# Cross-attention on one core: two of three value visits of a stage put side by side, and the work behind a visit reordered

## The chip, the core and the metric

The kernel runs on one core of a Trainium2 chip. The metric is device time in microseconds (us), from one launch to its end, as the median of several runs. On the core, TensorE (PE in the profile, its weight loads PEld) multiplies; VectorE (DVE), ScalarE (ACT) and GpSimd (POOL) work beside it; SyncE's queue (SPq) starts the DMAs. Each engine takes its instructions strictly in the order written, and they hold each other back by semaphores alone.

## The reference

A transformer block for 8 batch elements of 224 tokens of width 512, with 16 heads of 32: layer norms, masked self-attention, cross-attention over 750 context tokens, and a feed-forward net, all added to the input. What the change touches is the cross-attention:

```python
xs = _layernorm(src, ln2_g, ln2_b)
kv = xs @ ed_wkv
k2, v2 = (_heads(t) for t in jnp.split(kv, 2, axis=-1))
q2 = _heads(xq @ ed_wq)
wei2 = jnp.einsum('bhtd,bhjd->bhtj', q2, k2) * scale
wei2 = jax.nn.softmax(wei2, axis=-1)
ed_out = _merge(jnp.einsum('bhtj,bhjd->bhtd', wei2, v2)) @ ed_wproj + ed_bproj
result = result + ed_out
```

## The kernel before

Feed-forward and self-attention take about the first 750 us. Behind them comes the cross-attention, written as a plan: a list of named items, made by `plan_cross_attention`. Every engine walks the same list and issues its own part of each item, so the list is the order on all engines at once.

The work is cut into 32 groups of four heads (8 batch elements, 4 groups each). The 750 keys are six tiles of 125, taken as three pairs. The plan runs in stages. Stage s computes the keys of group s (items K), the score products of group s-1 (16 items "score", 112 queries by 376 keys, of which VectorE only takes the maxima, L1664), turns the maxima of group s-2 (M), computes the probabilities of group s-3 (12 items "prob": a head and a pair of key tiles each, two matmuls at L1744, which ScalarE exponentiates at L1607), and finishes group s-4. A stage has 12 slots. Slot i holds prob i, then a score product, then the fill of the slot (half of a K or of a value projection V, three to six matmuls at L1727; a part of an output projection E, three matmuls at L1832 for each; or T, three transposes of the next context, L1819), then further score products. I call a stage by s mod 4. Types 0 to 3 differ in their fill: type 0 has V, K and, from the third batch element on, E in slots 6, 7, 9 and 10, and none in 8 and 11; types 1 and 2 have none in slots 6 and 7 (type 1) or 7 (type 2) and none in 10 and 11; type 3 has a T in each slot from 4 to 11.

A "value visit" (item "value", L1773) multiplies one pair of key tiles with the values: eight matmuls whose results are 32 columns wide, one for each head and tile, four of them side by side in the array (the records show 16, two for each). Everything else in the loop uses 98 to 128 rows and up to 128 columns, M's two transposes apart. The visits of group s-3 stand at the end of slots 7 and 10 and, for the third pair, in slot 3 of the next stage, where the softmax denominators follow (item D, L1791, of the same shape). GpSimd adds up the probabilities for D (L1582, L1586), two additions behind slot 7 and two behind slot 11 of each stage; it also computes the low half of each T (L1473).

Three waits matter. A score product needs the third last user of its three banks to be read (L1757, L1758); a prob needs the exponential before the last (two banks, L1740, L1741); a visit needs its four exponentials (L1764). An E's last part is followed by an addition of the residual on VectorE (L1721), which stands before the maxima of the slot's last score products.

Of the kernel before, what the change touches and what calls it, by code (L numbers as in the profile page):

```python
# [636 lines left out]
def plan_attention(B):  # L637

    other = plan_cross_attention(B)
    start = other.index(FIRST_IN_TURN)  # L640
    early = [item for slot in EARLY.values() for item in slot]
    assert set(early) >= set(other[:start])
    items = []
    for item in plan_self_attention(B):
        if item[0] == "other_stage":
            items += [("ca",) + o for o in EARLY.get(item[1:], ())]
        else:
            items.append(("sa",) + item)
    behind = items.index(("sa", "T_split", 0, 1)) + 1
    items[behind:behind] = [("ff", "last")]  # L650
    return items + [("ca",) + o for o in other[start:] if o not in early]
# [623 lines left out]
VECTOR_SUMS = {3: (2,), 2: (1, 2), 1: (1,)}  # L1275
STATISTICS = ((1, 8), (1, 9), (1, 10), (1, 11), (2, 0), (2, 1))
OFFSET = (2, 3)


def plan_cross_attention(B):  # L1280

    NG = 4 * B
    items, late = [], []
    for s in range(-1, NG + 4):
        g, b = s % 4, s // 4
        fill = {i: [] for i in range(SLOTS)}  # L1290

        def put(slots, item, there):
            for part, i in enumerate(slots):
                if there:
                    fill[i].append(item + (part,))

        keys, now = 0 <= s < NG, 0 <= b < B
        if g == 0:
            put((0, 1), ("V", b, 0), now and b > 0)
            put((2, 3), ("K", s, 0), keys)  # L1300
            put((4, 5), ("K", s, 1), keys)
            put((7, 9), ("V", b, 0), now and b == 0)
            put((6, 6, 7, 7) if keys else (0, 0, 1, 1), ("E", b - 2, 0), 0 <= b - 2 < B - 1)
            put((9, 9, 10, 10), ("E", b - 2, 1), 0 <= b - 2 < B - 2)
        elif g == 1:
            put((0, 1), ("K", s, 0), keys)
            put((2, 3), ("K", s, 1), keys)
            put((4, 5), ("V", b, 1), now and b > 0)
            put((8, 9), ("V", b, 2), now)
        elif g == 2:  # L1310
            put((0, 1), ("K", s, 0), keys)
            put((2, 3), ("K", s, 1), keys)
            put((5, 6), ("V", b, 3), now)
            put((8, 9), ("V", b, 4), now)
        else:
            put((0, 1), ("K", s, 0), keys)
            put((2, 3), ("K", s, 1), keys)
            put((4, 5), ("V", b, 5), now)
            for n in range(8):
                if b + 1 < B:  # L1320
                    fill[4 + n].append(("T", b + 1, n % 4, n // 4))
        for i, c, m, part in LAST_E.get(s - NG, ()):
            fill[i].append(("E", B - c, m, part))
        for i in range(SLOTS):
            scores = []
            if 0 <= s - 1 < NG:
                scores = [("score", s - 1, u) for u in range(SCORED[g][i], SCORED[g][i + 1])]
            if 0 <= s - 3 < NG:
                items.append(("prob", s - 3, i))
            if i == 2 and 0 <= s - 2 < NG:  # L1330
                items.append(("M", s - 2))
            items += scores[:1]
            items += fill[i]
            items += late
            late = [("T_rest",) + item[1:4] for item in fill[i] if item[0] == "T"]
            items += [(item[0] + "_rest",) + item[1:3] for item in fill[i] if item[0] + str(item[3]) in ("K1", "E3")]
            if i == 3 and 0 <= s - 4 < NG:
                items.append(("value", s - 4, 2))
            divided = 3 if s <= NG else LAST_D
            for j, name in enumerate(("D", "", "D_high", "D_low") if s <= NG else ("D", "D_high", "D_low")):  # L1340
                if name and i == divided + j and 0 <= s - 4 < NG:
                    items.append((name, s - 4))
            items += scores[1:]
            if i == SLOTS - 1 and 0 <= s - 1 < NG:
                items.append(("negate", s - 1))
            if i % 4 == 3 and 0 <= s - 3 < NG and (s - 3, i) != (NG - 1, SLOTS - 1):
                items.append(("sum", s - 3, i))
            if i == 3 and keys:
                items.append(("queries", s))
            if i in (7, 10) and 0 <= s - 3 < NG:  # L1350
                items.append(("value", s - 3, (i - 7) // 3))
            if now and b + 1 < B:
                if b > 0 and (g, i) in STATISTICS:
                    items.append(("statistics", b + 1, STATISTICS.index((g, i))))
                if (g, i) == OFFSET:
                    items.append(("offset", b + 1))
                if g == 2:
                    items += [("normalise", b + 1, t) for t in range(CTX_TILES) if NORMALISE[t] == i]
                if (g, i) == (0, 11) and b > 0:
                    items += [("context", b + 1, a) for a in range(2)]  # L1360
        if g == 3 and 1 <= b < B - 1:
            items.append(("weights_low", b + 1))
        if g == 1 and 0 <= b - 2 < B - 1:
            items.append(("store", b - 2))
        if g == 2 and 0 <= b - 1 < B:
            items.append(("result", b - 1))
    return items
# [495 lines left out]
```

## Time and profile before

| | us |
|---|---|
| median of 3 runs | 1369.85 |
| lowest and highest run | 1369.48, 1372.99 |
| the profiled execution, span | 1372.2 |
| TensorE busy in it | 1310.9 |
| VectorE, GpSimd, ScalarE busy in it | 794.4, 701.5, 662.1 |

The rows further down come from the one profiled execution. In a timeline row the columns are: start, time from the start of the first to the end of the last of the instructions merged in it, engine, line, operation, result <- operands, shapes, count, and in brackets the idle time before it with what ended it. A matmul's record begins when it is issued and ends when its result is written, so records of matmuls overlap; two of them are compared here by their ends.

### The profile page before, as it was taken

To read this page: it belongs to the slowest core of one execution; us is meant where nothing else is said; L and a number is where in the kernel's file an instruction comes from. 1 tells how busy PE (TensorE), PEld (TensorE's weight loads), DVE (VectorE), ACT (ScalarE), POOL (GpSimd) and SP (SyncE) were. 2 spreads that over 40 slices of the span, in tenths; PEclk is the share of its full clock that TensorE was granted. 3 is DMA by queue.
4 is the path that set the end of the run, shared out by engine and by line. 5 is a ranking of instruction groups with operands and counts; after the bars stand their busy time and mean duration, and the time that the engine had idled before them with its cause. 6 is when DMAs were issued, how large, how long until landed. Compare 5 with 4: busy or idle time off the path is not lost.

```text
span 1372.2 us, 24578 instructions
## 1 busy us (share of the span) xinstructions
PE 1310.9 (96%) x9193; PEld 1082.5 (79%) x9193; DVE 794.4 (58%) x2007; ACT 662.1 (48%) x1609; POOL 701.5 (51%) x577
## 2 busy tenths in 40 slices
PE   7999999999899999998788999999999999999997
PEld 6888888888788888887677787878877787887874
DVE  6613223232777777776655575756757566575565
ACT  5311111232666665666433656474665647456444
POOL 3232221322444555556733767666676766667661
PEclk9999999999999999999599999999999999999999
DMA  7400102114647776547267685777677587766641
GB/s 237 145 18 16 62 31 77 46 60 117 139 86 178 166 186 148 122 123 185 63 142 119 100 128 98 132 123 125 101 127 120 101 137 104 142 101 112 90 71 41
DMA packets 100400, 151.67 MB, mean 111 GB/s; under 512 B 10197, under 2 KB 63229, under 8 KB 99514
## 3 DMA queue, kind: packets, MB, share of 16 engines
q1 hardware_dynamic: 100282, 150.11, 53.8%
q8 instruction: 73, 1.20, 0.4%
q14 instruction: 45, 0.37, 0.1%
HBM read 66.74 MB, written 24.12 MB: 66 GB/s over the span
## 4 chain that ended last, share of the span: by engine, by line
PE 76%; POOL 8%; issue 5%; DVE 5%; DMA 3%; ACT 2%; SPq 1%; POOLq 0%; ACTq 0%; DVEq 0%
PE ps L1727 18%; PE ps L453 11%; PE ps L164 10%; PE ps L423 10%; PE ps_pair L1744 6%; PE ps L1759 5%; PE ps L1773 5%; PE ps L1832 3%; POOL ca_partial L1586 2%; DMA ca_k_stack<-ca_keys 2%; POOL ca_xT L1473 1%; DMA sa_K_stack<-sa_rows 1%; PE ps L1207 1%; PE ps L1791 1%; PE ps L1227 1%
## 5 line engine op out<-in xcount | busy, mean ns | idle before, releaser
L1664 DVE TENSOR_REDUCE ca_maxes<-ps 112x1 f32<-112x375 f32 x512 | 256.5, 541 | 106.0 <-PE ps L1759 103.9
L1607 ACT ACTIVATE ca_probT<-ps_pair 125x448 f32<-125x448 f32 x384 | 210.3, 554 | 181.5 <-PE ps_pair L1744 179.6
L1586 POOL TENSOR_TENSOR ca_partial<-ca_partial,ca_probT 125x896 f32<-125x896 f32 x118 | 249.2, 2112 | 93.6 <-ACT ca_probT L1607 89.0
L312 POOL TENSOR_TENSOR ff_hT<-ff_hrelu,ff_hT 128x512 fp32r<-128x512 f32 (+1 forms) x64 | 77.9, 1218 | 203.2 <-DVE ff_hT L394 203.2
L1759 PE MATMUL ps<-ca_k_stack,ca_q_stack 96*112 96x376 f32 x512 | 168.7, 352 | 6.9 <-issue 3.6
L1744 PEld LDWEIGHTS ps_pair<-ca_q_stack,ca_k_stack 98*125 98x125 f32 x768 | 130.2, 186 | 44.0 <-issue 31.9
L1744 PE MATMUL ps_pair<-ca_q_stack,ca_k_stack 98*125 98x224 f32 x768 | 156.2, 285 | 1.3 <-ACT ca_probT L1607 1.2
L423 PE MATMUL ps<-ff_w,ff_hT 128*128 128x512 f32 x672 | 155.5, 390 | 0.0
L1727 PE MATMUL ps<-w_b,ca_xT 128*125 128x512 f32 x576 | 151.2, 398 | 3.1 <-POOL ca_xT L1473 2.5
L1727 PE MATMUL ps<-ca_xT,w_a 128*128 128x376 f32 x768 | 153.1, 335 | 0.0
L423 PEld LDWEIGHTS ps<-ff_w,ff_hT 128*128 128x128 f32 x672 | 125.6, 188 | 25.8
L1038 ACT ACTIVATE sa_prob<-sa_prob,sa_maxes 112x112 f32<-112x112 f32 (+1 forms) x256 | 109.2, 428 | 67.0 <-DVE sa_maxes L1112 66.9
L341 ACT ACTIVATE ff_hrelu<-ps,columns 128x512 f32<-128x512 f32 (+1 forms) x64 | 40.7, 636 | 200.9 <-PE ps L453 194.5
L1727 PEld LDWEIGHTS ps<-ca_xT,w_a 128*128 128x128 f32 x768 | 130.3, 189 | 0.6
L1112 DVE CUSTOM_DVE_ANT_0 sa_prob<-ps_pair,sa_masks 112x112 f32<-112x112 f32 (+1 forms) x256 | 74.5, 328 | 87.7 <-PE ps_pair L1197 86.2
L1727 PEld LDWEIGHTS ps<-w_b,ca_xT 128*125 128x125 f32 x576 | 105.7, 188 | 23.3 <-ACT ca_xT_f L1651 3.5
L394 DVE CAST ff_hT<-ff_hrelu 128x512 fp32r<-128x512 f32 (+1 forms) x64 | 27.8, 437 | 147.0 <-ACT ff_hrelu L341 146.8
L1582 POOL TENSOR_TENSOR ca_partial<-ca_probT 125x896 f32<-125x896 f32 x32 | 67.8, 2117 | 71.6 <-PE ps L1791 39.5
L1759 PEld LDWEIGHTS ps<-ca_k_stack,ca_q_stack 96*112 96x112 f32 x512 | 86.3, 177 | 20.0 <-DVE ca_maxes L1664 10.9
L1773 PE MATMUL ps<-ca_probT,ca_v 125*32 125x224 f32 x1536 | 92.6, 359 | 0.6 <-ACT ca_probT L1607 0.6
L1713 DVE TENSOR_TENSOR ca_keys<-ps,ca_keys 128x376 fp32r<-128x376 f32 x64 | 35.2, 550 | 77.5 <-ACT ca_keys L1640 77.5
L155 POOL TENSOR_TENSOR sa_rows<-sa_f,one 128x224 fp32r<-128x224 f32 x64 | 40.3, 629 | 76.0 <-ACT sa_f L1093 61.5
(145 smaller groups left out, 2433.0 us busy)
## 6 DMA issues: line engine op xcount, KB each, us to landing
ca_k_stack<-ca_keys SPq DMA_DIRECT2D x96, 376.0 KB, 8.0
sa_Q_stack<-sa_rows SPq DMA_DIRECT2D x96, 112.0 KB, 3.5
sa_K_stack<-sa_rows SPq DMA_DIRECT2D x96, 112.0 KB, 3.7
ca_q_stack<-q_out SPq DMA_DIRECT2D x96, 112.0 KB, 9.5
ctx_tokens<-in_ctx_dram SPq DMA_DIRECT2D x14, 672.0 KB
ctx_tokens<-in_L_xattn_ff_w_dram SPq DMA_DIRECT2D x16, 512.0 KB, 4.4
q_out<-sa_yT SPq DMA_DIRECT2D x16, 448.0 KB, 3.7
wp_lo<-wp_out SPq DMA_DIRECT2D x6, 1024.0 KB, 4.8
```

The costliest lines, as they stand in the source:

```text
L164: mm = pe.matmul(acc, lhs(a, k), rhs(b, k), start=n == 0, stop=n == len(steps) - 1)
L312: pool.tensor_tensor(hT[:, LO, m % RING, 0:width(g)], hrelu[i % 2][:, 0:width(g)], hT[:, HI, m % RING, 0:width(g)].bitcast(F32), ALU.subtr ...
L423: mm = pe.matmul(ps_y[t], hT[:, a, (KT * c + k) % RING, P * t:P * (t + 1)], w2[c][:, b, k, :], start=(c, k, a, b) == (0, 0) + PASSES[0], s ...
L453: mm = pe.matmul(ps_h[i % 2][:, 0:width(g)], w1[c][:, a, k, P * (m % KT):P * (m % KT + 1)], xT[:, b, k, tokens(g)], start=(k, n) == (0, 0) ...
L1038: ins = act.activation(prob[:, n % 4, TQ * q:TQ + T * q], prob[:, n % 4, TQ * q:TQ + T * q], ACT.Exp, bias=maxes[:, n % 4, q:q + 1], scale ...
L1586: pool.tensor_tensor(total, total, half(a), ALU.add).then_inc(partial_done, 1)
L1607: act.activation(probT[u // GH][0:JT, u % GH].rearrange("p a t -> p (a t)"), ps_p[u % 2][0:JT, 0:2 * T], ACT.Exp).then_inc(exp_done, 1)
L1664: dve.tensor_reduce(maxes[:, q, j, a:a + 1], ps_s[n % 3][0:TQ, 0:JH], AX_X, ALU.max).then_inc(s_read, 1)
L1727: mm = pe.matmul(acc, lhs(a, k), rhs(b, k), start=(k, i) == (0, 0), stop=(k, i) == (3, 2))
L1744: mm = pe.matmul(ps_p[n % 2][0:JT, T * i:T * (i + 1)], k_stack[:, h, t // 3, JT * (t % 3):JT * (t % 3 + 1)], q_stack[:, h, :], start=True, ...
L1759: pe.matmul(ps_s[n % 3][0:TQ, 0:JP], q_stack[0:KS, h, TQ * q:TQ * (q + 1)], k_stack[0:KS, h, a, :], start=True, stop=True).then_inc(s_psum, 1)
L1773: mm = pe.matmul(ps_o[HD * j:HD * (j + 1), 0:T], v[b % 2][:, t, HD * h:HD * (h + 1)], probT[pair][0:JT, j, i], start=t == 0, stop=t == NT - 1)
```

## The change

The first two pairs of key tiles meet the values in one place, at the end of slot 9, one visit directly behind the other. In slots 4 and 10, the slots that now follow visits, the slot's first score product stands ahead of the prob; where a stage has no score products left, the fill would stand there.

```diff
+VALUES_AT = 9
+BEHIND_VALUES = (4, VALUES_AT + 1)
...
-            if 0 <= s - 3 < NG:
-                items.append(("prob", s - 3, i))
-            if i == 2 and 0 <= s - 2 < NG:
-                items.append(("M", s - 2))
-            items += scores[:1]
-            items += fill[i]
+            prob = [("prob", s - 3, i)] if 0 <= s - 3 < NG else []
+            if i in BEHIND_VALUES:
+                items += (scores[:1] or fill[i]) + prob + (fill[i] if scores else [])
+            else:
+                items += prob
+                if i == 2 and 0 <= s - 2 < NG:
+                    items.append(("M", s - 2))
+                items += scores[:1] + fill[i]
...
-            if i in (7, 10) and 0 <= s - 3 < NG:
-                items.append(("value", s - 3, (i - 7) // 3))
+            if i == VALUES_AT and 0 <= s - 3 < NG:
+                items += [("value", s - 3, pair) for pair in range(2)]
```

The order moves on TensorE alone; on the other engines and on SyncE's queue the same instructions stand in the same order. TensorE, a type 0 stage, from the end of slot 7 to slot 11 (L1759 is a score product, L1744 a prob, L1832 a part of E, L1773 a value visit), before:

```order
1295 L1759 MATMUL ps<-ca_k_stack,ca_q_stack 112x376
1296 L1773 MATMUL ps<-ca_probT_112,ca_v_111 32x224 x8
1297 L1744 MATMUL ps_pair<-ca_q_stack,ca_k_stack 125x224 x2
1298 L1759 MATMUL ps<-ca_k_stack,ca_q_stack 112x376 x2
1299 L1744 MATMUL ps_pair<-ca_q_stack,ca_k_stack 125x224 x2
1300 L1759 MATMUL ps<-ca_k_stack,ca_q_stack 112x376
1301 L1832 MATMUL ps<-ca_wp_103,ca_oT_123 112x512
1302 L1832 MATMUL ps<-wp_lo,ca_oT_123 112x512
```

The same place now (all lines of this part of the file are 4 higher: L1763, L1748, L1836 and L1777):

```order
1299 L1763 MATMUL ps<-ca_k_stack,ca_q_stack 112x376
1300 L1748 MATMUL ps_pair<-ca_q_stack,ca_k_stack 125x224 x2
1301 L1763 MATMUL ps<-ca_k_stack,ca_q_stack 112x376 x2
1302 L1748 MATMUL ps_pair<-ca_q_stack,ca_k_stack 125x224 x2
1303 L1763 MATMUL ps<-ca_k_stack,ca_q_stack 112x376
1304 L1836 MATMUL ps<-ca_wp_103,ca_oT_123 112x512
1305 L1836 MATMUL ps<-wp_lo,ca_oT_123 112x512
```

The visit between the last score product of slot 7 and the prob of slot 8 is gone, and four score products follow with two probs between them and no other work.

TensorE, the end of slot 9 and slot 10 of a type 3 stage (L1819 is a T), before:

```order
1249 L1744 MATMUL ps_pair<-ca_q_stack,ca_k_stack 125x224 x2
1250 L1759 MATMUL ps<-ca_k_stack,ca_q_stack 112x376
1251 L1819 MATMUL ps<-ident,ctx_tokens 128x125 x3
1252 L1759 MATMUL ps<-ca_k_stack,ca_q_stack 112x376
1253 L1744 MATMUL ps_pair<-ca_q_stack,ca_k_stack 125x224 x2
1254 L1759 MATMUL ps<-ca_k_stack,ca_q_stack 112x376
1255 L1819 MATMUL ps<-ident,ctx_tokens 128x125 x3
1256 L1759 MATMUL ps<-ca_k_stack,ca_q_stack 112x376
```

The same place now:

```order
1250 L1763 MATMUL ps<-ca_k_stack,ca_q_stack 112x376
1251 L1823 MATMUL ps<-ident,ctx_tokens 128x125 x3
1252 L1763 MATMUL ps<-ca_k_stack,ca_q_stack 112x376
1253 L1777 MATMUL ps<-ca_probT_112,ca_v_111 32x224 x8
1254 L1777 MATMUL ps<-ca_probT_113,ca_v_111 32x224 x8
1255 L1763 MATMUL ps<-ca_k_stack,ca_q_stack 112x376
1256 L1748 MATMUL ps_pair<-ca_q_stack,ca_k_stack 125x224 x2
1257 L1823 MATMUL ps<-ident,ctx_tokens 128x125 x3
```

Both visits now stand between slots 9 and 10, and the score product of slot 10 comes before its prob.

## Rows read from the trace of the kernel before

**Rows 1.** The page: the chain that ended last, share of the span by engine

```profile
PE 76%; POOL 8%; issue 5%; DVE 5%; DMA 3%; ACT 2%; SPq 1%; POOLq 0%; ACTq 0%; DVEq 0%
```

**Rows 2.** Stages of type 3, 0, 1, 2: us, busy by engine, granted clock, DMA share, GB/s

```profile
983.15:1003.41 20.26, 19.50 (x159) 15.55 (x158) 12.09 (x24) 15.20 (x31) 14.70 (x10) 1.00 0.66 96
1003.41:1025.83 22.42, 22.07 (x161) 17.50 (x160) 12.35 (x24) 9.91 (x21) 15.26 (x11) 1.00 0.63 119
1025.83:1045.18 19.35, 19.33 (x149) 15.58 (x148) 12.52 (x25) 8.73 (x19) 11.23 (x6) 1.00 0.94 172
1045.18:1064.05 18.87, 18.87 (x149) 15.42 (x148) 14.42 (x36) 12.29 (x25) 12.57 (x7) 1.00 0.65 91
```

**Rows 3.** Timeline, type 0, TensorE: score then prob; the same around a visit

```profile
1021.78 0.34 PE L1759 MATMUL ps<-ca_k_stack,ca_q_stack 96*112 96x376 f32 x1
1021.96 0.38 PE L1744 MATMUL ps_pair<-ca_q_stack,ca_k_stack 98*125 98x224 f32 x2
...
1023.74 0.33 PE L1759 MATMUL ps<-ca_k_stack,ca_q_stack 96*112 96x376 f32 x1
...
1024.90 0.48 PE L1744 MATMUL ps_pair<-ca_q_stack,ca_k_stack 98*125 98x224 f32 x2
```

**Rows 4.** Timeline, type 1, TensorE: third visit (slot 3) with D behind it

```profile
1030.87 0.96 PE L1773 MATMUL ps<-ca_probT,ca_v 125*32 125x224 f32 x16
...
1031.65 0.56 PE L1791 MATMUL ps<-ca_partial,ca_ones 125*32 125x224 f32 x8
```

**Rows 5.** Timeline, type 0, slots 7 to 9: TensorE and VectorE

```profile
1018.17 0.33 PE L1759 MATMUL ps<-ca_k_stack,ca_q_stack 96*112 96x376 f32 x1
1018.37 0.69 DVE L1721 TENSOR_TENSOR ca_res<-ps,ca_res 112x512 f32<-112x512 f32 x1 [0.79 <-PE ps L1832]
...
1018.98 0.54 DVE L1664 TENSOR_REDUCE ca_maxes<-ps 112x1 f32<-112x375 f32 x1
```

**Rows 6.** Timeline, type 1, slots 6 and 7: VectorE's maxima, slot 7's two score products

```profile
1036.37 2.37 DVE L1664 TENSOR_REDUCE ca_maxes<-ps 112x1 f32<-112x375 f32 x5 [0.75 <-PE ps L1759]
...
1036.97 0.88 PE L1759 MATMUL ps<-ca_k_stack,ca_q_stack 96*112 96x376 f32 x2
```

**Rows 7.** Timeline, type 2, slots 6 and 7: the same

```profile
1056.25 1.46 DVE L1664 TENSOR_REDUCE ca_maxes<-ps 112x1 f32<-112x375 f32 x3 [0.69 <-PE ps L1759]
1056.27 0.50 PE L1759 MATMUL ps<-ca_k_stack,ca_q_stack 96*112 96x376 f32 x2
```

**Rows 8.** Timeline, type 3 and start of type 0: ScalarE, GpSimd, and TensorE behind them

```profile
997.57 0.98 POOL L1473 TENSOR_TENSOR ca_xT<-ca_xT_f,ca_xT 128x375 fp32r<-128x375 f32 x1 [0.22 <-ACT ca_xT_f L1651]
...
998.51 4.28 POOL L1586 TENSOR_TENSOR ca_partial<-ca_partial,ca_probT 125x896 f32<-125x896 f32 x2
...
999.38 0.41 PE L1759 MATMUL ps<-ca_k_stack,ca_q_stack 96*112 96x376 f32 x1
...
1001.91 0.64 ACT L1607 ACTIVATE ca_probT<-ps_pair 125x448 f32<-125x448 f32 x1
...
1003.87 1.63 PE L1727 MATMUL ps<-w_b,ca_xT 128*125 128x512 f32 x6 [0.35 <-POOL ca_xT L1473]
...
1006.53 4.30 POOL L1586 TENSOR_TENSOR ca_partial<-ca_partial,ca_probT 125x896 f32<-125x896 f32 x2
...
1010.89 0.58 PE L1791 MATMUL ps<-ca_partial,ca_ones 125*32 125x224 f32 x8
```

**Rows 9.** Timeline, the last two groups: exponentials on ScalarE, probs and last visit

```profile
1345.13 0.97 ACT L1607 ACTIVATE ca_probT<-ps_pair 125x448 f32<-125x448 f32 x2
...
1348.76 2.77 ACT L1607 ACTIVATE ca_probT<-ps_pair 125x448 f32<-125x448 f32 x5 [0.76 <-PE ps_pair L1744]
...
1355.82 0.48 PE L1744 MATMUL ps_pair<-ca_q_stack,ca_k_stack 98*125 98x224 f32 x2
...
1359.46 0.54 ACT L1607 ACTIVATE ca_probT<-ps_pair 125x448 f32<-125x448 f32 x1 [0.76 <-PE ps_pair L1744]
1360.06 0.96 PE L1773 MATMUL ps<-ca_probT,ca_v 125*32 125x224 f32 x16 [0.63 <-ACT ca_probT L1607]
```

## The prediction

> **What bounds the kernel now.** I read the chain of work that ended last first: three quarters of the span are TensorE's own work [rows 1]. Then busy time by stretch, over one period of the cross-attention, four stages, which repeats itself to some hundredths of a us from the second batch element to the seventh: stages of type 1 and 2 have TensorE busy for all but 0.02 us, type 0 for all but 0.35, type 3 for all but 0.76, with the clock granted in full, its level of 2.4 GHz [rows 2]. So a us taken off TensorE in types 1 and 2 is a us off the time, unless TensorE then waits for somebody. The next view is therefore the timeline around each place where a visit stood: who is late there if the visit is not.
>
> **What a visit costs.** Ends of records are compared. From the end of a score product to the end of the two matmuls of the next prob it takes 0.22 us without a visit (1022.12 to 1022.34) and 1.31 us with one (1024.07 to 1025.38) [rows 3]: a visit costs 1.09. Of this its own streaming is less. D, eight records in two sets of four, ends 0.38 behind the visit ahead of it (1031.83 to 1032.21) [rows 4]: 0.19 a set, and no loss between the two. A visit is four sets, 0.76. So 0.33 are lost around each visit, and a visit that directly follows another costs 0.76. The change takes one such loss from each of the 32 groups: 32 x 0.33 = 10.6 us of TensorE's time. The nearest row to the new edge, visit to visit, is the edge visit to D, same shape [rows 4], and I take it as it is.
>
> The Trainium skill, page "TensorEngine Tiling (Array Packing)", section "Key Properties", says that a change of the tiling mode drains TensorE while a change of tile does not; the trace agrees, with 0.33 lost around a visit and none between visit and D. By that rule alone the change would give all of the 10.6 us, about 1359.3; I weigh it as a rival.
>
> **The two reordered slots.** In slots 4 and 10 the score product goes first. Every matmul's own step depends on itself (score 0.17, a prob 0.22 for its two), and the loss at the end of a visit now falls on another instruction. I find no row with a score product behind a visit; bounds are that all or none of the exit's part of 0.33 goes, at most 0.33 either way for each. I take 0: the prob and what stands behind it end when they did. The prob reaches ScalarE 0.17 later and the score reaches VectorE 0.2 earlier.
>
> **Where the saving is taken back.** A score product waits for the third last user of its banks. In [rows 6] VectorE makes five maxima in 2.37 us, 0.54 each and so 0.46 apart. The second ends at 1037.37 and the second score product of slot 7, which waits for it, ends at 1037.85: release to end is 0.48. A visit (1.09) gave VectorE time; now the scores of the next slot come at once. Stage by stage:
>
> Type 0 with E fill (6 groups, batch elements 2 to 7). The residual addition of slot 7 keeps VectorE until about 1019; the maximum of slot 7's last score ends at 1019.52 [rows 5]. In the new order the scores behind it end at 1018.50 + 0.22 + 0.17 + 0.17 + 0.22 + 0.17 = 1019.45 for the first of slot 9, which is the third after that score and so may not end before 1019.52 + 0.48 = 1020.00. Wait 0.55. The fill behind it lets VectorE catch up. In slot 10 fill does that too. Net: -0.33 + 0.55 = +0.22.
>
> Type 1 (7 groups). Third maximum ends 1036.37 + 0.92 + 0.54 = 1037.83, so slot 8's first score may end at 1038.31; its own time would be 1037.85 + 0.22 + 0.17 = 1038.24: wait 0.07 [rows 6]. Behind the double visit, slots 10 and 11 are four scores and two probs without fill. Counted from the end of the first score, the fourth would end at 0.22 + 0.17 + 0.22 + 0.17 + 0.17 = 0.95, but the first one's maximum ends at 0.03 + 0.55 and frees it for 1.06: wait 0.11. Net: -0.33 + 0.07 + 0.11 = -0.15.
>
> Type 2 (7 groups). First maximum of three ends 1056.80, so slot 8's first score may end at 1057.28 against 1056.77 + 0.39 = 1057.16: wait 0.12 [rows 7]. Slots 10 and 11 as in type 1. Net: -0.33 + 0.12 + 0.11 = -0.10.
>
> Type 3 with T fill (7 groups). GpSimd is the bound here: the low half of a T from 997.57, the additions of the second pair 998.51 to 1002.79, four more low halves, and TensorE's V waits for the first of them at 1003.87; then the two additions of the third pair, 1006.53 to 1010.83, and D at 1010.89 [rows 8]. These start from ScalarE before slot 9 and don't move. Both removed and added visit lie inside. What TensorE gives to ScalarE must only not be late: from the end of slot 9's last score (999.79, [rows 8]) two visits and the score first take 1.31 + 0.76 + 0.17 = 2.24, so prob 10 ends at 1002.03 where ScalarE began on it at 1001.91: 0.13 late, inside GpSimd's cover, which the V at 1003.87 (the prob ahead of it still ends 0.25 before) keeps. If the cover were gone, 0.13 to 0.76 for each of 7. I take 0.
>
> Stages without T or E fill (the second group, G = 1, and the fourth from the end, G = 28) are bound by VectorE from slot 7 on. Two breaks of 1.47 from a score to the next score behind a visit, less the 1.33 or so of maxima still queued and in hand, become one of 2.0: from the end of slot 7 to slot 11, 5.1 us become 4.9. Net -0.20 each. G = 29 is like type 1: -0.15.
>
> The last two groups have no scores. TensorE feeds ScalarE with probs alone, two ahead at most, 0.43 apart when queued (0.97 for two, 0.54 for one) [rows 9]. Group 30: prob 8 waits for an exponential that ends 1345.67, and ends 1346.2; prob 9 1346.6; two visits and prob 10, 1.31 + 0.76 = 2.07, 1348.7; the last exponential starts 0.43 behind, at 1349.15, and not at 1348.76: +0.40. Group 31: prob 8 ends 1356.2 in place of 1356.30, then 0.70 of E, 0.22, 0.70 of E, 2.07: 1359.9, the last exponential starts 1360.3 and not at 1359.46, and the last visit (1360.06) waits for it: +0.84 [rows 9].
>
> **The sum.** 6 x 0.22 - 7 x 0.15 - 7 x 0.10 + 7 x 0 - 2 x 0.20 - 0.15 + 0.40 + 0.84 = 1.32 - 1.05 - 0.70 - 0.40 - 0.15 + 1.24 = +0.26 us. The sum is made against the profiled execution, whose span is 1372.2 us; that one lies 2.35 us above the median of 1369.85 and near the highest of the three runs. A difference carries over: 1369.85 + 0.26 = 1370.1. About 0.3%, or 4.1 us, is what a measurement of this kernel can tell from no change.
>
> **The rivals.**
>
> A, the gain stays. If VectorE frees the banks in time in the stages of type 0, 1 and 2 and only type 3 is covered, 24 or so groups x 0.33 = 7.9 us: 1362.0; with type 3 and the ends too, all 32, 1359.3. That last number is where the drain rule of the Trainium skill named above would put it by itself. For it: TensorE's busy share in types 1 and 2 [rows 2]. Against: the maxima are 0.46 apart and a slot without fill has two of them in 0.56 us of TensorE's time, so two such slots in a row must stall [rows 5 to 7].
>
> B, the double visit starves those behind it. During 2.07 us TensorE gives ScalarE and GpSimd nothing, and in type 3 ScalarE works without a pause, 1.5 us a slot. If ScalarE's 0.13 (or up to 0.76, a whole visit, if its queue is empty when the visit starts) gets into the chain of GpSimd's low halves, and if the wait of type 0, 0.55, also arises in types 1 and 2: 7 x 0.76 + 14 x 0.45 - 1.4 + 1.2 = about +11, half of it +5: 1375 to 1381. It decides from the point where prob 10's exponential is on GpSimd's path. Against: GpSimd has 4 us of additions queued [rows 8].
>
> C, score first pays or costs. If the exit is cheaper before a score product by half its 0.19, 2 x 0.1 x 25 stages = -5: 1365; dearer likewise 1375. Against: in a stretch of its own nothing suggests that the loss knows its successor.
>
> D, the change doesn't reach TensorE as written: excluded by the order, where it alone moves.
>
> **Chances.** Forecast (savings and waits cancel, within 1.5 us) 0.72. A 0.08, C faster 0.03 and slower 0.03, B 0.06, and 0.08 for the forecast with one term off by some us on either side but within 0.3%. Together: faster by over 0.3% 0.11, within 0.80, slower 0.09. The range for 8 in 10: the forecast's own case is 1368.5 to 1371.6; the runs shown scatter by 3 us upward, and the terms' bounds (7 x 0.3 in type 3, 14 x 0.1 elsewhere) add some 3 us either way: 1366.5 to 1373.5.
>
> **What would show it.** In the profile after: visits come in pairs with records 0.17 to 0.19 apart and no idle weight load between them; idle time of weight loads before L1777 falls by a third. In type 0, the first score of slot 9 waits about 0.5 us for a maximum; types 1 and 2 show waits of about 0.1 in slot 8 and 11; four stages take about 80.9 us as before (22.64, 19.2, 18.77, 20.26). The last exponential comes about 1.2 us nearer to the end. The forecast is wrong if the four stages' period moves by more than 0.5 us, since there are six or seven of them; the first place to look at would be type 3, where I rest on a cover.

## The result and the profile after

The changed kernel takes 1376.88 us in the median of 15 runs (1373.25 to 1381.53), the kernel before, in 15 runs beside them, 1371.03 (1367.48 to 1374.93). The ratio is 1.0043 with a 95% interval of 1.0033 to 1.0053: 5.9 us slower, between 4.5 and 7.3. I had forecast +0.26 us, with a range up to 1373.5; the change is slower, by more than 0.3%, to which I had given 9 chances in 100.

The two profiled executions hide it: 1371.9 us after, 1372.2 before. The execution after is among the three fastest of its kernel's 15 (1374.37 us timed, so 2.5 us more than its span). The one before has a span that is already above the median time of its kernel, 1371.03. The stretch before the first prob took 739.5 us in one and 743.1 in the other, with the same order of TensorE's instructions. Of these 3.6 us, some 2.4 arise between 650 and 700 us; from 652 to 683 us the granted clock was 0.78 after and 0.50 before. So what follows compares stages, which repeat to some hundredths of a us. A stage is counted from the end of its first prob's first matmul to the same point of the next stage. Busy time by stretch of the changed kernel, one period, stages of type 3, 0, 1 and 2 (columns: stretch, its length, busy time of TensorE, weight loads, VectorE, ScalarE, GpSimd with counts, granted clock, DMA share, GB/s; to be held against [rows 2]):

```profile
980.79:1001.13 20.34, 19.43 (x159) 15.66 (x158) 11.98 (x24) 15.49 (x32) 14.79 (x10) 1.00 0.64 92
1001.13:1023.69 22.56, 22.00 (x160) 17.80 (x160) 11.83 (x24) 9.87 (x21) 15.18 (x11) 1.00 0.58 115
1023.69:1042.98 19.29, 19.27 (x148) 15.71 (x148) 13.01 (x26) 8.84 (x19) 11.29 (x6) 1.00 0.98 181
1042.98:1062.18 19.20, 19.03 (x149) 15.50 (x148) 14.43 (x36) 11.95 (x23) 12.60 (x7) 1.00 0.64 89
```

Against 20.26, 22.42, 19.35 and 18.87 before that is +0.08, +0.14, -0.06 and +0.33: 81.39 us for four stages in place of 80.90. I had written 22.64 for type 0, 19.2 for type 1, 20.26 for type 3 and 18.77 for type 2. Three are within 0.1; type 2, where I forecast a gain of 0.10, lost 0.33, and that six times over. The period moved by 0.49, at the edge of the 0.5 that I had named as the sign of being wrong.

The chain that ended last shows the same from afar: TensorE's share fell from 76% [rows 1] to 69%, and VectorE's and ScalarE's rose.

```profile
PE 69%; POOL 9%; DVE 7%; issue 6%; DMA 4%; ACT 4%; SPq 1%; POOLq 0%; ACTq 0%; DVEq 0%
```

The waits of the weight loads, whole span, show what was bought and with what: first of before, then of after (engine and line that waited <- releaser: us in total, times, longest).

```profile
PEld ps_pair L1744 <- issue: 31.9, 89, 0.4
PEld ps L1773 <- issue: 19.6, 81, 0.3
PEld ps L1759 <- DVE ca_maxes L1664: 10.9, 28, 1.4
...
PEld ps_pair L1744 <- ACT ca_probT L1607: 5.2, 13, 0.7
```

```profile
PEld ps L1763 <- issue: 24.8, 60, 2.3
PEld ps L1763 <- DVE ca_maxes L1668: 14.3, 36, 1.4
PEld ps L1777 <- issue: 13.6, 51, 0.3
...
PEld ps_pair L1748 <- ACT ca_probT L1611: 8.7, 21, 0.9
```

The idle time on either side of a visit is put down to issue. It was 31.9 + 19.6 = 51.5 us. In the changed kernel it moved from the prob to the score product, which is now first behind a visit; but 4.0 of the 24.8 lie ahead of the first visit, as they do before the change. Counted from 757 us on, where the visits begin, it is 20.8 + 13.4 and 1.7 at the probs, 35.9 us: it fell by three tenths. Waits for maxima and for exponentials rose by 3.4 and 3.5. Weight loads are ahead of their matmuls, so these sums are not times of the kernel; they say where to look.

**Type 0, slots 7 to 9**, the timeline of the changed kernel (start, duration, engine, line, result <- operands):

```profile
1015.82 0.34 PE L1763 MATMUL ps<-ca_k_stack,ca_q_stack 96*112 96x376 f32 x1
1015.99 0.38 PE L1748 MATMUL ps_pair<-ca_q_stack,ca_k_stack 98*125 98x224 f32 x2
1016.02 0.69 DVE L1725 TENSOR_TENSOR ca_res<-ps,ca_res 112x512 f32<-112x512 f32 x1 [0.79 <-PE ps L1836]
1016.21 0.51 PE L1763 MATMUL ps<-ca_k_stack,ca_q_stack 96*112 96x376 f32 x2
...
1016.56 0.38 PE L1748 MATMUL ps_pair<-ca_q_stack,ca_k_stack 98*125 98x224 f32 x2
1016.63 1.90 DVE L1668 TENSOR_REDUCE ca_maxes<-ps 112x1 f32<-112x375 f32 x4
1017.22 0.43 PE L1763 MATMUL ps<-ca_k_stack,ca_q_stack 96*112 96x376 f32 x1 [0.29 <-DVE ca_maxes L1668]
```

The residual addition holds VectorE until 1016.7, the first of four maxima ends at 1017.17, and the score product that waits for it is issued at 1017.22. The prob before it ended at 1016.94 and the score at 1017.65, 0.71 apart where 0.17 is its own: a wait of 0.54, where I had 0.55.

**Type 2, slots 6 to 8**, the same kernel:

```profile
1051.87 0.38 PE L1748 MATMUL ps_pair<-ca_q_stack,ca_k_stack 98*125 98x224 f32 x2
...
1053.45 0.82 ACT L1617 ACTIVATE ctx_tokens<-ctx_tokens,ca_shift,ctx_ln_rstd 125x512 f32<-125x512 f32 x1
...
1054.07 0.51 PE L1763 MATMUL ps<-ca_k_stack,ca_q_stack 96*112 96x376 f32 x2
1054.16 0.53 ACT L1611 ACTIVATE ca_probT<-ps_pair 125x448 f32<-125x448 f32 x1
...
1054.74 0.48 PE L1748 MATMUL ps_pair<-ca_q_stack,ca_k_stack 98*125 98x224 f32 x2 [0.17 <-ACT ca_probT L1611]
```

Here it is not the score product that waits for VectorE but the prob ahead of it, for ScalarE. Exponential 6 runs until 1054.69, the prob of slot 8 is issued 0.05 later and ends at 1055.22; the two score products of slot 7 ended at 1054.58, so 0.64 lie where a prob takes 0.22: 0.43 lost before rounding. The matmuls of prob 6 had ended at 1052.25, but ScalarE did other work first, last a layer-norm pass of 0.82 us.

**Behind a double visit**, the end of type 2 and the first prob of type 3:

```profile
1060.48 0.42 PE L1763 MATMUL ps<-ca_k_stack,ca_q_stack 96*112 96x376 f32 x1
1060.74 0.38 PE L1748 MATMUL ps_pair<-ca_q_stack,ca_k_stack 98*125 98x224 f32 x2
...
1060.95 0.33 PE L1763 MATMUL ps<-ca_k_stack,ca_q_stack 96*112 96x376 f32 x1
...
1061.13 0.38 PE L1748 MATMUL ps_pair<-ca_q_stack,ca_k_stack 98*125 98x224 f32 x2
1061.15 0.54 ACT L1611 ACTIVATE ca_probT<-ps_pair 125x448 f32<-125x448 f32 x1 [1.09 <-PE ps_pair L1748]
...
1061.34 0.63 PE L1763 MATMUL ps<-ca_k_stack,ca_q_stack 96*112 96x376 f32 x2
...
1061.84 0.45 PE L1748 MATMUL ps_pair<-ca_q_stack,ca_k_stack 98*125 98x224 f32 x2
```

The fourth score product ends at 1061.97, 1.07 behind the first one (1060.90) where 0.95 would be its own: 0.11, as forecast. Then the prob of the next slot 0 ends at 1062.29, 0.32 behind and not 0.22: its weight load waits for exponential 10, which runs to 1061.69 since its prob now stands behind a score product. That 0.10 I had left out.

### The profile page after: what moved, and what is told of

Its sections match the earlier page's. It is cut to its first block, busy times and chain, and to the rows that moved or that the text cites. A ratio compares the mean times of both kernels' runs of the same rounds, so it can differ in the third digit from the quotient of the medians.

```text
span 1371.9 us, 24578 instructions
## 1 busy us (share of the span) xinstructions
PE 1304.6 (95%) x9193; PEld 1083.2 (79%) x9193; DVE 792.6 (58%) x2007; ACT 661.9 (48%) x1609; POOL 703.5 (51%) x577
## 4 chain that ended last, share of the span: by engine, by line
PE 69%; POOL 9%; DVE 7%; issue 6%; DMA 4%; ACT 4%; SPq 1%; POOLq 0%; ACTq 0%; DVEq 0%
PE ps L1731 16%; PE ps L453 11%; PE ps L423 10%; PE ps L164 9%; PE ps L1763 5%; PE ps L1777 5%; PE ps_pair L1748 5%; PE ps L1836 3%; DMA ca_k_stack<-ca_keys 2%; POOL ca_partial L1590 2%; POOL ca_xT L1477 1%; DMA sa_K_stack<-sa_rows 1%; DVE ca_oT_f L1709 1%; PE ps L1795 1%; POOL sa_fin L1029 1%
## 5 line engine op out<-in xcount | busy, mean ns | idle before, releaser
L1611 ACT ACTIVATE ca_probT<-ps_pair 125x448 f32<-125x448 f32 x384 | 205.7, 547 | 189.6 <-PE ps_pair L1748 188.0
L1763 PE MATMUL ps<-ca_k_stack,ca_q_stack 96*112 96x376 f32 x512 | 180.1, 369 | 8.7 <-DVE ca_maxes L1668 4.4
L1748 PE MATMUL ps_pair<-ca_q_stack,ca_k_stack 98*125 98x224 f32 x768 | 148.5, 277 | 3.5 <-ACT ca_probT L1611 3.5
L1748 PEld LDWEIGHTS ps_pair<-ca_q_stack,ca_k_stack 98*125 98x125 f32 x768 | 132.5, 187 | 18.7 <-ACT ca_probT L1611 8.7
L1763 PEld LDWEIGHTS ps<-ca_k_stack,ca_q_stack 96*112 96x112 f32 x512 | 88.3, 176 | 46.5 <-issue 24.8
L1777 PE MATMUL ps<-ca_probT,ca_v 125*32 125x224 f32 x1536 | 85.9, 357 | 0.9 <-ACT ca_probT L1611 0.9
```

Of the source, the lines that this page charges most:

```text
L1611: act.activation(probT[u // GH][0:JT, u % GH].rearrange("p a t -> p (a t)"), ps_p[u % 2][0:JT, 0:2 * T], ACT.Exp).then_inc(exp_done, 1)
L1748: mm = pe.matmul(ps_p[n % 2][0:JT, T * i:T * (i + 1)], k_stack[:, h, t // 3, JT * (t % 3):JT * (t % 3 + 1)], q_stack[:, h, :], start=True, ...
L1763: pe.matmul(ps_s[n % 3][0:TQ, 0:JP], q_stack[0:KS, h, TQ * q:TQ * (q + 1)], k_stack[0:KS, h, a, :], start=True, stop=True).then_inc(s_psum, 1)
L1777: mm = pe.matmul(ps_o[HD * j:HD * (j + 1), 0:T], v[b % 2][:, t, HD * h:HD * (h + 1)], probT[pair][0:JT, j, i], start=t == 0, stop=t == NT - 1)
```

## The experiments

All kernels below differ from the changed kernel, or from the one before where that is said, in the plan alone. Stage lengths are those of one period of each profile, types 3, 0, 1 and 2.

**The prob first again behind visits.**

```diff
-BEHIND_VALUES = (4, VALUES_AT + 1)
+BEHIND_VALUES = ()
```

> The changed kernel with the merged visits, but the prob ahead of the score product in slots 4 and 10, as before the change. In the profile of the changed kernel four stages take 81.40 us. Theory 1 (score first spreads VectorE's maxima): behind the double visit the fourth score product waits about 0.33 instead of 0.11 us, the prob of the next slot 0 no longer waits its 0.11, together +0.11 in types 1 and 2: four stages 81.6 us. Theory 2 (score first only delays the exponential that the next slot 0 waits for): 0.11 less in each of types 2 and 3, four stages 81.2 us.

Measured: 20.37, 22.54, 19.44, 19.34, together 81.69 us; its one run took 1379.02 us. Types 1 and 2 are 0.15 and 0.14 longer than in the changed kernel.

```profile
1027.54:1046.98 19.44, 19.32 (x148) 15.71 (x148) 12.91 (x26) 8.96 (x19) 11.39 (x7) 1.00 0.96 178
1046.98:1066.32 19.34, 19.09 (x149) 15.54 (x148) 14.44 (x36) 12.24 (x24) 12.46 (x7) 1.00 0.65 92
```

Its timeline behind the double visit:

```profile
1064.50 0.47 PE L1748 MATMUL ps_pair<-ca_q_stack,ca_k_stack 98*125 98x224 f32 x2
...
1064.81 0.51 PE L1763 MATMUL ps<-ca_k_stack,ca_q_stack 96*112 96x376 f32 x2
...
1065.18 1.91 DVE L1668 TENSOR_REDUCE ca_maxes<-ps 112x1 f32<-112x375 f32 x4 [1.68 <-PE ps L1763]
...
1065.37 0.84 PE L1763 MATMUL ps<-ca_k_stack,ca_q_stack 96*112 96x376 f32 x2
1065.78 0.17 PEld L1763 LDWEIGHTS ps<-ca_k_stack,ca_q_stack 96*112 96x112 f32 x1 [0.34 <-DVE ca_maxes L1668]
```

VectorE begins 0.2 us later, counted from the visits, and the last score product waits 0.34 instead of 0.11; the prob of slot 0 no longer waits. Theory 1 holds: the reordering is worth 0.23 - 0.10 = 0.13 in each of types 1 and 2, 0.15 and 0.14 by the stages. It is the part of the change that helps, given the merged visits; I had put it at nothing. The loss at the end of a visit is the same before either successor: from the end of the last visit to the end of the second item behind it, score and prob, it takes 0.57 us in the changed kernel, and here, prob and score, 0.58.

**The layer-norm passes later.**

```diff
-NORMALISE = (4, 5, 6, 7, 9, 10)
+NORMALISE = (6, 8, 9, 9, 10, 11)
```

> The changed kernel with the six layer-norm passes of type 2 stages on ScalarE moved from slots 4, 5, 6, 7, 9, 10 to slots 6, 8, 9, 9, 10, 11. Theory 1 (prob 8 of type 2 waits 0.43 us because ScalarE comes to exponential 6 late, behind layer-norm passes, now that no visit stands between): the wait falls to the 0.12 that VectorE asks for, four stages 81.40 - 0.31 = 81.1 us, and 2 us less in all. Theory 2 (the wait has another cause, the matmuls themselves or VectorE): four stages stay at 81.4 us, the same time as the changed kernel.

Measured: 20.35, 22.53, 19.26, 18.93, together 81.07. In time: 1374.26 us against 1371.51 for the kernel before, ratio 1.0021 (1.0010 to 1.0032).

```profile
1045.62:1064.55 18.93, 18.93 (x149) 15.66 (x148) 14.43 (x36) 11.59 (x22) 12.59 (x7) 1.00 0.65 92
```

Of the repeating stages type 2 alone moves by more than 0.04, by 0.27, and TensorE has no idle time left in it. In slot 8 the prob takes its own 0.22 again, and the score product behind it waits the 0.12 for VectorE. So the 0.43 were ScalarE's order of work. In time the loss is 2.8 us instead of 5.9, 3 less where 2 were expected. (Group 0 took 22.34 us in this profile and 20.90 in the changed kernel's; the granted clock in it was 0.92 here and 1.00 there.)

**The double visit of type 0 in slot 8.**

```diff
-VALUES_AT = 9
+VALUES_AT = (8, 9, 9, 9)
...
-            if i in BEHIND_VALUES:
+            if i in (4, VALUES_AT[g] + 1):
```

> The changed kernel with the double visit of type 0 stages at the end of slot 8 instead of slot 9 (and the score product first in slot 9). Theory 1 (the loss of type 0 is the 0.54 us wait for VectorE, which works on the residual): the visit gives VectorE its time, the wait in slot 9 goes, type 0 takes 22.56 - 0.54 = 22.0 us, four stages 80.9, some 3 us less in all than the changed kernel. Theory 2 (the merged visit itself loses more than the separate ones): type 0 stays at 22.5 us.

Measured: 20.35, 22.04, 19.25, 19.21, together 80.85. In time: 1373.91 against 1371.51, ratio 1.0021 (1.0010 to 1.0033).

```profile
1003.70:1025.74 22.04, 21.75 (x161) 17.74 (x160) 11.80 (x24) 9.89 (x21) 15.20 (x11) 1.00 0.61 117
```

0.52 less in type 0 than in the changed kernel, and the wait in slot 9 is gone. A visit one slot earlier stands between the busy VectorE and the scores that would wait for it. Group 29, in a type 0 stage too but without that addition, doesn't gain: 16.01 us against 15.39.

**The visits of type 0 apart.** Type 0 has them in slots 7 and 10 as before, the other types keep the double visit.

```diff
-VALUES_AT = 9
+VALUES_AT = ((7, 10), (9, 9), (9, 9), (9, 9))
...
-            if i in BEHIND_VALUES:
+            if i == 4 or (i == 10 and g > 0):
...
+                items += [("value", s - 3, pair) for pair in range(2) if VALUES_AT[g][pair] == i]
```

> The changed kernel with the two visits of type 0 stages back in slots 7 and 10; merged in types 1, 2 and 3. Theory 1 (losses are local to the stage in which VectorE is late): type 0 takes 22.42 us as before the change, without a wait in slot 9, the other three keep 19.3, 19.2 and 20.3, four stages 81.25 us. Theory 2 (the stages hand their delay on to each other): type 0 does not return to 22.4, or the others move.

Measured: 20.35, 22.35, 19.25, 19.24, together 81.19; its one run took 1376.49 us.

```profile
1002.79:1025.14 22.35, 22.06 (x160) 17.56 (x160) 12.38 (x25) 9.89 (x21) 15.20 (x11) 1.00 0.63 119
```

The loss is local to the stage. 22.35 and not 22.42, because the type 3 stage ahead hands over 0.08 late to a wait that absorbs it: the V of slot 0 waits for GpSimd at a fixed time.

**The residual addition behind the maxima.** The changed kernel, with VectorE's addition of an output projection moved behind the maxima of the slot's last score products.

```diff
-            items += [(item[0] + "_rest",) + item[1:3] for item in fill[i] if item[0] + str(item[3]) in ("K1", "E3")]
+            items += [("K_rest",) + item[1:3] for item in fill[i] if item[0] + str(item[3]) == "K1"]
...
             items += scores[1:]
+            items += [("E_rest",) + item[1:3] for item in fill[i] if item[0] + str(item[3]) == "E3"]
```

> The changed kernel with VectorE's residual addition of an output projection behind the maxima of its slot's last score products instead of ahead of them. Theory 1 (the 0.54 us wait of the first score product of slot 9 in type 0 is the maximum that stands behind the 0.69 us addition): that maximum ends 0.44 us earlier, the wait falls to about 0.1, type 0 takes 22.56 - 0.44 = 22.1 us, four stages 80.95, 2.6 us less in all. Theory 2 (four score products close together are too many for VectorE with or without the addition): the wait stays near 0.5.

Measured: 20.35, 22.13, 19.25, 19.20, together 80.93; 1374.68 us against 1371.05, ratio 1.0026 (1.0015 to 1.0038).

```profile
1015.83 0.55 DVE L1669 TENSOR_REDUCE ca_maxes<-ps 112x1 f32<-112x375 f32 x1 [0.96 <-PE ps L1764]
...
1016.30 0.68 DVE L1726 TENSOR_TENSOR ca_res<-ps,ca_res 112x512 f32<-112x512 f32 x1
...
1016.44 0.43 PE L1764 MATMUL ps<-ca_k_stack,ca_q_stack 96*112 96x376 f32 x1
```

The maximum now ends at 1016.38, ahead of the addition; the score product of slot 9 is issued at 1016.44 and ends at 1016.87, 0.12 late instead of 0.54. So it was the addition that made 0.42 of the 0.54, not the number of score products.

**The last two groups apart.** Visits of groups 30 and 31 in slots 7 and 10 again.

```diff
+APART = 2
...
+        visits = (VALUES_AT, VALUES_AT) if s - 3 < NG - APART else (7, 10)
...
-            if i in BEHIND_VALUES:
+            if i == 4 or (i == VALUES_AT + 1 and visits[0] == VALUES_AT):
...
+                items += [("value", s - 3, pair) for pair in range(2) if visits[pair] == i]
```

> The changed kernel with the visits of the last two groups (30 and 31) apart again in slots 7 and 10. Theory 1 (these groups have no scores to fill ScalarE's time with, the double visit costs them 0.40 + 0.84 us): some 1.2 us less than the changed kernel, group 30's probabilities from first to the next group's first 9.8 instead of 10.6 us. Theory 2 (the end is set by the DMA and the last output projection): no difference.

Measured: group 30 takes 9.71 us from its first prob to the next group's (10.63 in the changed kernel, 9.79 before), and from there to the end of TensorE's work 18.69 (19.09 after). Together 1.3 us, as forecast. In time 1375.28 against 1370.91, ratio 1.0028 (1.0014 to 1.0043). ScalarE's last two exponentials in the changed kernel, in one row behind a pause of 2.21 us, and then the same two here:

```profile
1359.71 0.98 ACT L1611 ACTIVATE ca_probT<-ps_pair 125x448 f32<-125x448 f32 x2 [2.21 <-PE ps_pair L1748]
```

```profile
1359.59 0.54 ACT L1612 ACTIVATE ca_probT<-ps_pair 125x448 f32<-125x448 f32 x1 [0.37 <-PE ps_pair L1749]
1360.89 0.54 ACT L1612 ACTIVATE ca_probT<-ps_pair 125x448 f32<-125x448 f32 x1 [0.76 <-PE ps_pair L1749]
```

**Late passes in the kernel before.** The same edit of NORMALISE, without the change.

> The kernel before with the layer-norm passes of type 2 stages in slots 6, 8, 9, 9, 10, 11. Theory 1 (with a visit in slot 7 exponential 6 is in time anyway): nothing moves, type 2 stays at 18.87 us, four stages at 80.90. Theory 2 (the passes as such cost time there): type 2 falls by 0.1 to 0.3 us.

Measured: 20.26, 22.42, 19.35, 19.35, together 81.38; its one run took 1377.56 us. Neither theory had this: type 2 is 0.48 longer.

```profile
1047.11:1066.46 19.35, 19.10 (x149) 15.37 (x148) 14.90 (x37) 11.70 (x23) 12.58 (x7) 1.00 0.66 95
```

```profile
1064.03 1.52 ACT L1613 ACTIVATE ctx_tokens<-ctx_tokens,ca_shift,ctx_ln_rstd 125x512 f32<-125x512 f32 x2
...
1065.45 0.53 ACT L1607 ACTIVATE ca_probT<-ps_pair 125x448 f32<-125x448 f32 x1
1065.88 0.81 ACT L1613 ACTIVATE ctx_tokens<-ctx_tokens,ca_shift,ctx_ln_rstd 125x512 f32<-125x512 f32 x1
...
1066.12 0.45 PE L1744 MATMUL ps_pair<-ca_q_stack,ca_k_stack 98*125 98x224 f32 x2 [0.25 <-ACT ca_probT L1607]
```

Here no double visit stands behind slot 9, and ScalarE isn't through its two passes in time; exponential 10 comes at 1065.45, and the prob of the next slot 0 ends 0.69 behind the score product ahead of it instead of 0.22. An order of ScalarE's work is good or bad only beside a place of the visits.

**Each double visit where its stage has work queued.** Late passes, and visits by stage type; apart in type 3 and for the last three groups. The score product stands ahead of the prob only behind the double visit of type 0.

```diff
-VALUES_AT = 9
-BEHIND_VALUES = (4, VALUES_AT + 1)
+VISITS = {0: (8, 8), 1: (10, 10), 2: (10, 10), 3: (7, 10)}
+APART = 3
...
+        visits = VISITS[g] if s - 3 < NG - APART else (7, 10)
...
+            if i == 9 and visits == (8, 8):
...
+                items += [("value", s - 3, pair) for pair in range(2) if visits[pair] == i]
```

> Merged visits put where VectorE and ScalarE have work queued: at the end of slot 8 in type 0 stages (score product first in slot 9), of slot 10 in types 1 and 2; apart, as before the change, in type 3 and for the last three groups; layer-norm passes of type 2 in slots 6, 8, 9, 9, 10, 11. Theory 1 (each merge gives back 0.33 us and each wait is what VectorE's 0.46 us a maximum makes of it): type 0 22.0, type 1 19.35 - 0.33 + 0.07 = 19.1, type 2 18.87 - 0.33 + 0.12 = 18.7, type 3 20.26 as before, four stages 80.0 to 80.1 and so 5 us less than the kernel before, 8 less than the changed one. Theory 2 (a double visit always hands its saving back as waits): four stages not under 80.8.

Measured: 1365.68 us against 1370.91 for the kernel before, ratio 0.9963 (0.9948 to 0.9978), the fastest of all. The period:

```profile
976.83:997.09 20.26, 19.50 (x160) 15.55 (x158) 12.07 (x24) 15.72 (x32) 14.71 (x10) 1.00 0.67 98
997.09:1019.18 22.09, 21.74 (x161) 17.67 (x160) 11.77 (x23) 9.91 (x21) 15.27 (x11) 1.00 0.60 117
1019.18:1038.27 19.09, 19.06 (x148) 15.74 (x148) 13.52 (x27) 8.73 (x19) 11.25 (x6) 1.00 0.97 175
1038.27:1056.96 18.69, 18.69 (x148) 15.67 (x148) 13.81 (x35) 11.86 (x24) 12.60 (x7) 1.00 0.66 94
```

80.13 us for four stages. Types 1 and 2 are 19.35 - 0.33 + 0.07 and 18.87 - 0.33 + 0.12 to within 0.03, which is the surest measure of the 0.33 that a merged visit gives. The rows agree: a single visit ends 0.89 us behind the score product ahead of it, a double one 1.65, so the second costs 0.76 and not 1.09. The merging is a gain where nobody is late behind it. Against the changed kernel the gain is 5.2 + 5.9 = 11 us, not the 8 expected.

**The same with the passes where they were.**

> As the run with visits placed by stage type, but with the layer-norm passes where they were (slots 4, 5, 6, 7, 9, 10). Theory 1 (prob 8 of type 2 then waits for exponential 6 by 0.43 us): type 2 takes 19.0 us, 0.3 more than with the late passes; the others the same. Theory 2 (the wait comes from the visits' merging in slot 9): type 2 at 18.7 as with the late passes.

Measured: 20.28, 22.09, 19.08, 18.99, together 80.44; its one run took 1368.77 us.

```profile
1040.32:1059.31 18.99, 18.82 (x149) 15.54 (x148) 13.84 (x35) 12.59 (x25) 12.60 (x7) 1.00 0.66 96
```

0.30 more in type 2: the wait for exponential 6 is there as soon as the visit of slot 7 is gone, wherever it went.

## Why the prediction was wrong

The mechanism was right in kind, savings against waits, but the sum left out two waits for ScalarE and undervalued one for VectorE, and what was left out is most of the loss.

What a visit costs, 1.09, and what merging gives, 0.33: right (the placed version shows it in two stage types). The drain rule of the Trainium skill ("TensorEngine Tiling (Array Packing)", "Key Properties") held as far as TensorE alone goes (0.33 us saved for each change of mode that fell away, 0.76 us for a visit directly behind a visit); the 1359 us that it would give by itself did not come, since the instructions that moved up had to wait for others.

Type 0, -0.33 + 0.55 = +0.22: right, the wait is 0.54 as measured, and its cause is shown by moving the addition. The stage shows +0.14, since it begins 0.08 late and the wait of V in slot 0 takes that up.

Type 1, -0.33 + 0.07 + 0.11 = -0.15: both waits measured as written. The term left out is the prob of the next slot 0, +0.10. Stage: -0.06.

Type 2, -0.33 + 0.12 + 0.11 = -0.10: the step that failed. I took from the timeline how late VectorE was in slot 8 and didn't ask the same of ScalarE for the prob that stands ahead of that score product: the term for it was nothing, without a reason. It waited 0.43 for exponential 6, and the 0.12 for VectorE vanished behind that. With 0.11 and the 0.10 of the next slot 0 it makes -0.33 + 0.43 + 0.11 + 0.10 = +0.31; measured +0.33, in six stages: 0.43 each more than I wrote, 2.6 us of the miss. That the wait and the miss of a stage are the same number is chance: the wait replaced my 0.12, and the 0.10 came on top. The seventh, group 27, has no next context to normalise; it takes 18.88 us and waits 0.12 in slot 8, which is the forecast's own term.

Type 3, 0: nearly. Exponential 10 starts 0.13 later than before, counted from the stage's begin, as written. The cover held: the V of slot 0 starts 20.72 us into the stage before and 20.73 after. Inside it TensorE is 0.08 later: its transposes of slot 9 end 16.5 us into the stage in both kernels, but behind them it now works without a wait where it had one in slot 10, and is through at 20.34 instead of 20.26. The V's wait takes that up.

"Score first: I take 0": mis-sized in both directions. Behind the double visit it costs 0.10 at the next slot 0 and saves 0.23 at the fourth score product.

Group 29, which I set like type 1 at -0.15: +0.22 (15.39 against 15.17): its score product in slot 8 waits 0.37 for VectorE, where I had 0.07, and the 0.10 at the next prob comes on top. The last two groups: +1.24 forecast and 1.3 measured by taking them apart. Counted between first probs it lies the other way round from what I wrote, +0.84 in group 30 and +0.40 behind it.

Against my terms, type 2 lost 2.7 us more than forecast, type 1 0.8, group 29 0.4 and all else 0.15. Adding what the profile shows from the first prob of group 0: +0.26 in groups 0 to 3, +2.70 in groups 4 to 27, -0.11, +0.22 and +0.84 in 28 to 30. The rest after that is 0.86 shorter in the changed kernel's profile, though its last exponential is later; there the clock differs between the two executions. The last 6 us, before and then after:

```profile
1366.00:1372.00 6.00, 2.78 (x6) 1.54 (x6) 1.65 (x3) 0.00 (x0) 0.00 (x0) 0.76 0.25 76
```

```profile
1366.00:1372.00 6.00, 1.64 (x6) 0.97 (x6) 2.13 (x6) 0.28 (x1) 0.00 (x0) 1.00 0.24 76
```

The last six output matmuls took 2.90 us in one and 1.64 in the other. With that taken out, the profiles differ by 3.05 + 1.26 = 4.3 us, just under the 4.5 to 7.3 of the timed runs. The other 1.5 us of the median's 5.9 seem to go with the granted clock of whole runs. The three runs of the changed kernel with a mean clock of 0.990 took 1374.26 us in the median; 15 runs of the kernel before with 0.990 or more, measured beside the experiments, took 1370.10: 4.2 us, as the stages say. But 7 of 15 runs of the changed kernel have a mean clock of 0.986 or less (1376.4 to 1381.5 us), and 5 of 52 of the kernel before (1372.5 to 1375.2). Whether the change brings the lower clock on, or the sessions differed, is not shown.

The rivals: B, the slower one, has the measured time in its range of 1375 to 1381, but by chance; it named the right engine in the wrong stage. It looked for a starving ScalarE behind the double visit in type 3; it was a ScalarE short of time in type 2, where a single visit had been taken away. A, that the gain stays, is what the placed version reaches in good part for types 1 and 2. C, that a score product first pays or costs at the exit of a visit, is refuted by the two sums of 0.57 and 0.58 us above.

## What to carry to other kernels

A piece of work that keeps one engine busy and asks nothing of the others is also a breathing space for the others: whoever moves it must ask, for every instruction that now comes earlier, what each of its semaphores waits for, and not only the one that was last before. A merge that saves a switch pays where the instructions behind its old places have slack, so place it by stage, not once for all; here the merge was +5.9 us in one place for all and -5.2 us placed by stage, left out in type 3 and at the end, with ScalarE's passes moved along (0.3 us of the 0.8 us a period; in the kernel before, those passes alone cost 0.48). Where profiled executions scatter by more than the effect, compare repeating stages and not spans.

## What the runs showed of the hardware

The granted clock at the very end differed between executions: after the same 2.51 us pause of TensorE ahead of the last output projection, it fell to the lower of its two levels, 1.2 GHz, for a part of the time in five of the eleven profiles (0.76 over the last 6 us in the kernel before, matmuls of 0.63 us) and stayed at 2.4 GHz in six (1.00 in the changed kernel, matmuls of 0.39 us). That alone moves the time by 1.3 us.

A reduction of VectorE lasts 0.54 us in its row, but the next begins 0.46 behind its start, and the weight load of the score product that waits for it starts 0.05 behind the end of the row (1017.17 to 1017.22): the rate goes by the one number, the wait by the other. Forecasts with both came within 0.01 us of the measured 0.54, 0.07 and 0.11.
